# Routing batch 0 inside the last attention items, the shared expert of chunk 1 behind the routed blocks, and one closing step for the last chunk

## The reference, cut to what matters

```python
x = _layernorm(x + _L1_attn_ref(x, ...))            # heads of 16, causal softmax
# _L1_ffn_ref
scores = softmax(einsum('th,eh->te', xf, gate_w))   # 8 experts
topk_w, topk_i = top_k(scores, 2)
topk_w = topk_w / sum(topk_w)
y = sum over the 2 chosen experts of topk_w * (silu(xf @ wg[e]) * (xf @ wu[e])) @ wd[e]
shared = silu(xf @ sg) * (xf @ su) @ sd             # every token
x = _layernorm(x + y + shared)
```

## Time and profile before

| | |
|---|---|
| median of 3 runs (lowest to highest) | 717.64 us (717.23 to 723.69) |
| profiled execution | 718.89 us, of it 717.1 us span |
| PE busy in the span | 648.1 us, 90% |
| DVE busy | 412.5 us, 58% |
| ACT busy | 394.5 us, 55% |
| POOL busy | 233.0 us, 32% |
| mean granted clock of PE | 0.931 |

### The profile page before, as it was taken

The page is one execution under the profiler, slowest core; times in us unless marked ns, Lnnn a source line. Parts: engine busy times, 40 slices in busy tenths (PEclk is TensorE's granted clock), DMA queues, the critical chain, the costliest instruction groups (busy, mean ns, idle before and its releaser), DMA issues. The chain is left out here.

```text
span 717.1 us, 11088 instructions
## 1 busy us (share of the span) xinstructions
PE 648.1 (90%) x3717; PEld 301.7 (42%) x3717; DVE 412.5 (58%) x1069; ACT 394.5 (55%) x565; POOL 233.0 (32%) x255
## 2 busy tenths in 40 slices
PE   4998899999998979999969999999999889999870
PEld 1654422222431344445422222243344657877450
DVE  1478616334466696979451333245738846547697
ACT  1235679988586832545438888867775133333100
POOL 0002533335412223113341344523122705325250
PEclk9998599999998989879898999999999999999996
DMA  8500143333224422310415545433570253575331
GB/s 276 168 0 16 43 74 54 58 57 57 39 37 68 67 71 70 67 53 1 67 32 86 83 79 84 81 64 62 90 225 1 97 190 126 175 235 164 102 119 59
DMA packets 52105, 62.68 MB, mean 87 GB/s; under 512 B 10150, under 2 KB 38819, under 8 KB 51891
## 3 DMA queue, kind: packets, MB, share of 16 engines
q1 hardware_dynamic: 48971, 53.50, 33.1%
q0 software_dynamic: 3072, 8.39, 3.8%
HBM read 28.79 MB, written 18.35 MB: 66 GB/s over the span
## 5 line engine op out<-in xcount | busy, mean ns | idle before, releaser
L1411 ACT ACTIVATE probs<-ps 128x1024 f32<-128x1024 f32 (+1 forms) x320 | 276.2, 963 | 67.6 <-PE ps L1329 67.5
L1329 PE MATMUL ps<-ops_mem 99*128 99x512 bf16 (+3 forms) x768 | 165.7, 338 | 10.8 <-issue 6.8
L1346 PE MATMUL ps<-probs,vstat 128*32 128x512 f32 (+3 forms) x1536 | 169.0, 512 | 7.1 <-DVE raw L1251 6.3
L1422 POOL TENSOR_SCALAR_AFFINE_SELECT probs<-probs 128x512 f32<-128x512 f32 x128 | 84.6, 661 | 210.6 <-ACT probs L1411 210.0
L1329 PEld LDWEIGHTS ps<-ops_mem 99*128 99x128 bf16 x768 | 58.3, 99 | 159.8 <-ACT probs L1411 86.3
L1251 DVE COPY raw<-ps 128x512 f32<-128x512 f32 x32 | 22.1, 691 | 141.9 <-PE ps L1346 141.7
L1346 PEld LDWEIGHTS ps<-probs,vstat 128*32 128x32 f32 x1536 | 31.3, 109 | 70.9 <-issue 47.6
L2278 PE MATMUL ps<-parts_mem 128*128 x184 | 47.4, 381 | 0.3 <-ACT parts_mem L2159 0.3
L2122 POOL DMA_INDIRECT yT<-made,w1qkv x32 | 30.5, 954 | 47.0 <-DMA made<-parts_mem 37.8
L2113 POOL DMA_INDIRECT sent<-xres,w1qkv x32 | 30.8, 964 | 39.8 <-DVE w1qkv L615 22.2
L1720 PE MATMUL ps<-ops_mem,w1qkv 128*128 128x512 f32 x64 | 36.4, 698 | 0.1
(11 more groups left out here) (214 smaller groups left out, 937.3 us busy)
## 6 DMA issues: line engine op xcount, KB each, us to landing
ops_mem<-parts_mem SPq DMA_DIRECT2D x276, 64.0 KB
sent<-in_zero_row SPq DMA_DIRECT2D x2, 2944.0 KB, 67.9
made<-parts_mem SPq DMA_DIRECT2D x46, 128.0 KB, 1.8
probs<-sent SPq DMA_DIRECT2D x4, 896.0 KB, 8.8
ops_mem<-parts_mem SPq DMA_DIRECT2D x66, 32.0 KB
yT<-in_xT SPq DMA_DIRECT2D x4, 512.0 KB, 7.6
xres<-in_x SPq DMA_DIRECT2D x1, 2048.0 KB, 14.5
parts_mem<-in_wgu SPq DMA_DIRECT2D x2, 1024.0 KB
```

The lines of the kernel that those rows point to most:

```text
L1329: last = nc.tensor.matmul(ps[:, bank, o:o + CH - lo], kT[0:KDIM, buf, h if kh == GH else 0, kt * P:(kt + 1) * P], qT[0:KDIM, buf, h, c * C ...
L1346: last = nc.tensor.matmul(ps[32 * h:32 * h + 32, AV, lo:CH], vstat[:, i % 2, kt, h if kh == GH else 0, :], probs[:, s % PRING, h, 0:CH - l ...
L1411: nc.scalar.activation(o, banks, ACT.Exp, scale=score_scale).then_inc(s_exp, 1)
L1422: nc.gpsimd.affine_select(out=block_, in_=block_, compare_op=ALU.is_ge, fill=0.0, base=0, pattern=[[0, GH], [1, P]], channel_multiplier=-1 ...
```

## The change

It does three things.

1. **Batch 0 is routed within the attention.** The uses of bank 7 move to earlier steps: the second projection of chunk 1 from (5, 6) to (5, 4), the turns of chunk 0 from (5, 11) and (6, 2) to (5, 10) and (6, 2), its logits stay at (6, 4), the turns of chunk 1 come at (6, 6) and (6, 8) and its logits at (6, 10), in place of (6, 11), (7, 2) and (7, 4). `shift` moves behind them into item 6, ACT's `exp` from (7, 8) to (7, 1), `choose` before `take(7, 0)`, `rank` to (7, 8) in bank 7 as use 10, and `keep_rank` and `seat` before `take(7, 1)`. For this the norm of chunk 1 moves from the middle of item 6 to the end of item 5, ahead of both copies of chunk 0's turned rows. The three small tensors that `rank` and `seat` read are loaded ahead of the experts' weights, under a semaphore of their own.
2. **The shared expert of chunk 1** (`gate_up` 2 and 3, `down` 1, with their silu, product and sum) moves from before the blocks to behind them. `weigh(1)` comes into the loop at iterations 43 and 44, and chunk 0's weighing, statistics and scaling come two iterations earlier.
3. **The last chunk** ends in one sum, one norm and one store of four tiles. Weighing now comes ahead of the shared expert's sum for chunks 1 to 3, and takes the residual in with its first product.

The diff, cut to its core:

```diff
             def beside(self, pe, i, s):
-                for m, steps in enumerate((((4, 8), (4, 10)), ((5, 2), (5, 6)))):
+                for m, steps in enumerate((((4, 8), (4, 10)), ((5, 2), (5, 4)))):
                     if (i, s) in steps:
                         self.project(pe, m, steps.index((i, s)))
-                for m, steps in enumerate((((5, 11), (6, 2)), ((6, 11), (7, 2)))):
+                for m, steps in enumerate((((5, 10), (6, 2)), ((6, 6), (6, 8)))):
                     if (i, s) in steps:
                         self.turn(pe, m, steps.index((i, s)))
-                if (i, s) in ((6, 4), (7, 4)):
+                if (i, s) in ((6, 4), (6, 10)):
...
+                if (i, s) == (7, 8):
+                    pe.wait_ge(self.s_chosen, 1)
+                    pe.wait_ge(s_rank_w, 48)
+                    self.seven(pe, self.RANKS)
+                    self.rank(pe, 0, 7).then_inc(self.s_seven, 1)
             def before(self, dve, i):
                 if i == 5:
                     self.sum(dve, 1, 0)
+                    self.sum(dve, 1, 1)
                 if i == 6:
-                    self.of.k.then(self.of.statistics(0, y_sums[1]))
-                if i >= 6:
-                    self.evicted(dve, self.LOGIT[i - 6])
-                    self.keep_logits(i - 6, 7).then_inc(self.s_evicted, 1)
+                    self.keep_turned(dve, 0, 1)
+                    self.keep_seven(dve, 0)
+                if i == 7:
+                    self.choose(dve, 0)
             def between(self, dve, i):
...
                 if i == 5:
-                    self.sum(dve, 1, 1)
-                if i in (5, 6):
                     self.of.scale()
-                    self.of.apply(x_of(i - 5)).then_inc(self.s_norm, 1)
-                    self.keep_turned(dve, i - 5, 0)
+                    self.of.apply(x_of(0)).then_inc(self.s_norm, 1)
+                    self.norm(dve, 1)
+                    self.of.k.then(self.of.statistics(0, y_sums[1]))
+                if i == 6:
+                    self.keep_turned(dve, 1, 0)
+                    self.keep_turned(dve, 1, 1)
+                    self.keep_seven(dve, 1)
+                    self.shift(dve, 0)
                 if i == 7:
-                    self.shift(dve, 0)
-                    self.choose(dve, 0)
+                    self.evicted(dve, self.RANKS)
+                    self.keep_rank(7).then_inc(self.s_evicted, 1)
+                    dve.wait_ge(self.s_evicted, self.RANKS + 1)
+                    self.seat(dve, 0)
             def behind(self, dve, i):
...
                 if i == 5:
-                    self.norm(dve, 1)
-                if i in (5, 6):
-                    self.keep_turned(dve, i - 5, 1)
+                    self.of.scale()
+                    self.of.apply(x_of(1)).then_inc(self.s_norm, 1)
+                    self.keep_turned(dve, 0, 0)
...
-                        if route and (i, s) == (NI - 1, 8):
+                        if route and (i, s) == (NI - 1, 1):
                             route.exp(act, 0)
...
                 route.exp(act, 1)
-                silu(2)
-                silu(3)
...
                 bank_free(pe)
+                route.seven(pe, route.RANKS + 1)
                 project(2)
                 pe.wait_ge(s_exp_w, 16 * len(expert_weights))
-                route.rank(pe, 0)
...
                 logits(3)
-                gate_up(2)
-                gate_up(3)
-                down(1)
...
+                gate_up(2)
+                gate_up(3)
                 gate_up(4)
+                down(1)
                 gate_up(5)
...
                 route.shift(dve, 1)
-                multiplied(2)
-                multiplied(3)
                 route.choose(dve, 1)
-                accumulate(1)
                 for n in range(NB_ALL + 2):
...
-                    if n == 38:
+                    if n == 36:
                         weigh(0, (0, 1))
+                    if n == 37:
+                        weigh(0, (2, 3))
                     if n == 39:
-                        weigh(0, (2, 3))
-                    if n == 41:
                         of = normalised(0, range(CT))
                         statistics(of)
+                    if n == 41:
+                        scaled(of, 0)
                     if n == 43:
-                        scaled(of, 0)
+                        weigh(1, (0, 1))
+                    if n == 44:
+                        weigh(1, (2, 3))
+                multiplied(2)
+                multiplied(3)
                 multiplied(4)
-                weigh(1, range(CT))
+                accumulate(1)
                 multiplied(5)
...
-                for n, (lo, hi) in enumerate(LAST):
...
-                    weigh(3, range(lo, hi))
-                    of = normalised(3, range(lo, hi))
-                    statistics(of)
-                    scaled(of, 3)
+                weigh(3)
+                accumulate(3)
+                of = normalised(3, range(CT))
+                statistics(of)
+                scaled(of, 3)
```

More of the change, by code:

```diff
@@ L2367, in _, with weigh @@
                 end = Count(dve, s_dve_end)
-                def weigh(c, tiles):
+                def weigh(c, tiles=range(CT)):
                     dve.wait_ge(s_back[c], 16 * CT * TOP)
-                    if c < NC - 1:
-                        dve.wait_ge(s_dve_tail, dve_at["sum", c])
                     for k in range(TOP):
@@ L2414, in _ @@
                     if n == 3:
-                        route.keep_rank(dve, 1)
+                        dve.wait_ge(route.s_ranked, 1)
+                        route.k.then(route.keep_rank(5))
                     if n < NB_ALL:
@@ L2437, in _ @@
                 multiplied(6)
+                weigh(2)
                 accumulate(2)
-                weigh(2, range(CT))
                 multiplied(7)
```

104 lines of the change are left out of this document (48 added, 56 removed).

## The result

The changed kernel took 729.94 us (median of 20 runs, 721.83 to 734.12) against 721.43 us for the kernel before beside it: ratio 1.0131, 95% interval 1.0099 to 1.0163. On the median of 717.64 us that is 9.4 us more (7.1 to 11.7); 10.7 had been forecast. The ratio is estimated from the executions that ran at the usual clock, and is not the quotient of the two medians (1.012). On another chip, later, the same two kernels gave 1.0181 (1.0146 to 1.0215). The profiled execution has a span of 728.4 us, 11.3 more than before.

What follows compares the result with a forecast made beforehand. PE bounds layer 1's attention and the blocks, DVE the end; 8.8 + 3.7 - 12.1 + 2.7 + 1.5 + 1.7 + 4.4 = +10.7 us on 717.64 gives 728.3 us, range 721 to 734 leaving out 2 in 10.

Steps and rivals of the forecast that it cites:

- The wait at (6, 2): Attention: PE waits 6.5 us at chunk 0's second turn for a copy standing behind chunk 1's scale and apply.
- Rival B: No long wait at (6, 2), the turn needing only chunk 0's norm: 714.3 us, or down to 709.9; chance 0.06.
- Item 7: Attention: PE waits 2.3 us before the values of step 4, as `choose` stands before `take(7, 0)`.
- PE's clock: Lower clock behind the two attention waits: 2.4 us behind (6, 2), 1.3 us behind item 7, 3.7 together.
- Rival A: Waits come, but the clock does not fall and DVE catches up in the loop: +5.2, 722.8 us; chance 0.22.
- the four terms: Attention: waits of 6.5 and 2.3 us plus clock terms of 2.4 and 1.3 us.
- Ahead of the blocks: From `gate_up` 2 to the first block: chunk 1's shared expert moved away saves 12.1 us.
- The scatter: POOL's scatter of batch 0 and the first block load finish before PE reaches the blocks, hidden by 5 us.
- The first blocks: PE waits 2.7 us for ACT's copy, then DVE's `hidden`, with `choose` uncovered; 1.5 us of lower clock added.
- `weigh(1)` in the loop: Blocks near the loop's end: two halves of `weigh(1)` cost PE 1.7 us, bounds 0.6 and 3.4.
- The end: Behind the blocks: +3.1 us to DVE's last instruction and +1.3 us for the larger store, 4.4 together.
- Rival C: Lower clock lasts 3 us at each of three places, `weigh(1)` uncovered, gathered rows late: +17.2, 734.8 us; chance 0.12.

Runs made afterwards that it cites:

- experiment 1: Kernel after with both copies of chunk 0's turned rows ahead of chunk 1's scale and apply on DVE; ratio to before 0.9968.
- experiment 5: On top of experiment 1: in item 7 `choose` behind `take(7, 0)`, rank one scores step later, `seat` ahead of the last `normalise`; ratio to before 0.9970.
- experiment 10: Experiment 8 with the item 7 reordering of experiment 5 taken back, `choose` again ahead of `take(7, 0)`; ratio to before 0.9922.
- experiment 11: The repetition: kernel after once more, unchanged, on one chip with experiment 12; ratio to before 1.0181.
- experiment 12: Experiment 9's kernel once more, on one chip with the kernel after; ratio to before 1.0049.
- part 1 alone: Kernel before with only the routing of batch 0 moved into the attention; ratio to before 1.0217, +15.6 us.
- experiment 9: Kernel after with PE repeating the scores of step (6, 3) 27 times in the wait at (6, 2); ratio to before 1.0103.
- Experiment 4: Kernel after with part 1 taken back, leaving parts 2 and 3; ratio to before 0.9999.
- experiment 6: Kernel after with PE repeating the scores of step (6, 3) 17 times in the wait at (6, 2); ratio to before 1.0159.
- experiment 3: Kernel before with only part 3's single closing (sum still ahead of weighing); ratio to before 0.9971, -2.1 us.
- experiment 7: Experiment 1 with chunk 1's shared expert back ahead of the blocks, one closing kept; ratio to before 0.9947, -3.8 us.
- Experiment 8: Experiment 5 with `gate_up` 2 and 3 back ahead of the blocks, only `down` 1 behind them; ratio to before 0.9933, -4.8 us.

## Why the prediction was right

**The wait at (6, 2)**: 6.5 us forecast, 6.41 measured, on the copy and for the reason given. (The prediction's 512.15 is 512.12 by its own terms, which changes nothing.) Rival B is out: the turn did not run at once, and with the copies put first (experiment 1), which makes B's case but for item 7, the time is 717.64 - 2.3 = 715.3 us, where B gave 714.3.

**Item 7**: 2.3 us of wait forecast, 1.33 measured. Most of the difference is `choose`: DVE did it from 546.61 to 550.48 + 0.22, 4.1 us, where the step took 4.7 from the earlier trace rows. The wait made no difference that the runs can tell (experiments 5 and 10).

**PE's clock**: 2.4 and 1.3 us forecast. The first term was too small. Against the profile of before, which lost 1.6 us behind the logits itself, it measured 3.2, and 4.5 in the repetition; against work that does not fall at all, 4.8 to 6.1. Its bound of 3 us came from a low stretch of which only 6 us had been seen. The second was 0 in one execution and 1.5 in another. Rival A, no fall, is out: the fall is in the trace at (6, 2), experiments 11 and 12 show that it costs time, and A's 722.8 us, a ratio of 1.007, lies below both intervals. Together the four terms made 12.5; the stage grew by 11.7 in the profile, 0.4 of it for rank, and part 1 alone cost 15.6 by the runs.

The Trainium skill, TensorE: Matmul & The Clock Gate, section HAM oscillation, takes half the throttled time as the penalty and makes no deduction for idle time in it. In the wait itself (509.6 to 516.01) the granted clock was 0.75 on average, so part of it was low; yet the wait, which DVE ends, was as long as with PE busy at 1.00 in experiment 9 (6.41 us against 6.48). Only the work behind it grew. The measurement decides for the prediction's way of counting, though not for its size.

**Ahead of the blocks**: -12.1 forecast, -12.7 measured; the first block at 590.45, with 3.3 us of the profile's offset in it. The scatter was hidden, as forecast: the first block load was issued at 584.60, 5.9 us ahead of the first block. Experiment 4 shows that this holds only with part 1.

**The first blocks**: 2.7 us of wait and 1.5 of clock forecast, 4.2 together. Measured: a wait of 1.01 us on ACT, where before it was 0.33, and none on `hidden`. From the first block's turn to rank it took 9.5 us against 5.8, +3.7, so some 3 us of it is the lower clock. That the slow products are what let DVE catch up was not tested; in experiments 1 and 6 PE did wait for `hidden`, 0.24 and 0.40 us. The sum was right, its division was not: the two terms cover each other.

**`weigh(1)` in the loop**: 1.7 forecast; the rest of the blocks grew from 78.3 to 79.4, 1.1 us. The term stood for PE waiting for the weighing, and that is not where it went: PE's waits there went from 4.9 to 5.1 us only, and its busy time grew by 1.0 (73.3 to 74.3). A wait of 2.08 us at 671.85 is followed by products of 1.44 and 1.82 us in place of 1.03; before, a wait of 2.31 us at 669.21 was followed by one product of 2.01 us in place of 1.29.

**The end**: +4.4 forecast, +4.1 measured; DVE's last instruction 725.09 - 679.37 = 45.7 us behind the blocks, 45.9 forecast, and the store 3.3 us where 3.4 was forecast. (The prediction's 27.5 us for DVE's last stretch add up to 27.3 by its own terms.) But the heading it stood under was wrong. One closing shortens the end by 5.4 us in the profile (experiment 3); chunk 1's work, moved there, lengthens it by 49.0 - 39.5 = 9.5. So part 2 removes 12.7 us ahead of the blocks and puts 9.5 behind them and 3.7 to 4.9 into them: nothing is left, as experiments 4 and 7 say.

**Why the terms came to the right sum.** By stages, forecast and profile are +12.5 and +11.7 for the attention, -12.1 and -12.7 ahead of the blocks, +5.9 and +4.9 for the blocks, +4.4 and +4.1 for the end: 10.7 and 8.0 together. The runs gave 9.4, and 13.0 the second time, so the forecast lies between the two measurements. The big terms, the wait, the work moved and the end, were right for their reasons. Inside the stages there was luck: the clock behind (6, 2) was 1 to 2 us too small against a kernel before that loses 1.6 us there itself, and up to 4 against one that does not, while item 7 was 1 us of wait and 1.3 of clock too large, and in the blocks a wait too large by 2 stood beside a clock term too small by 1.5. The second measurement is nearer to the larger clock term. Rival C had the mechanism of the longer fall, but at all three places and with the other covers gone as well; its +17.2 us lies above both measurements.

**What beats both kernels.** Copies first, one closing, half of chunk 1 ahead of the blocks (experiment 10): ratio 0.9922 (0.9897 to 0.9947), 712.0 us on the median of before. Experiment 8 is level with it.

Two things stay open. Experiment 9 should lie above experiment 1 by about its repeats, 6.2 us of work. It lies 9.7 us above it, and its repetition, experiment 12, 5.8 (7.4 and 3.5 above the kernel before); each is known to some 3 us, and what more there is to the spread is not explained. And whether the 1 us of item 7 arrives in the runs was not found out.

## What to carry to other kernels

When an operation is moved among steps on one engine, follow the buffer that it frees: here two copies of 0.7 us, put behind 4 us of scaling, held a bank that TensorE needed, and nothing could make the time up. Count such a wait of the busiest engine at up to double its length, since the work behind it runs slower; and measure each part alone and taken back alone, because two parts may be without gain alone (part 2) or be worth only as cover for another (part 1).

## What was unexpected of the hardware

The granted clock falls in different places from one execution of the same program to the next: behind the wait of 1.3 us in item 7 it fell in two profiles (1.64 and 1.69 us for eight values) and not in five others (1.06 or 1.07). It also falls behind the narrow logits, with no long wait near. Of the ten profiles without a long wait at (6, 2), four have a fall of some 1.6 us behind the logits of chunk 0 and six have none. And `down(0)`, which follows logits of 8 columns and a wait of 1.16 us, took 3.70 us in seven of the fourteen profiled executions and 5.07 to 6.42 in the other seven; in three of these the logits themselves were already slow (2.59 to 2.76 us in place of 1.95). Whether there the narrow products or the short wait ahead of them bring it about was not tested.

Single profiles of this kernel therefore differ by some 3 us in stages that are alike, and a term of that size needs repeated runs. Over a longer stretch it is more: PE's 2588 instructions ahead of the change, which are alike in all fourteen kernels, took 479.8 to 488.4 us in the profiles.

Filling the wait of 6.4 us with useless products made the kernel faster than leaving TensorE idle in it: by 1.3% on a common chip, and by 0.3%, which is not clear of zero, in a comparison across chips. Filling it in part (3.97 us, 2.50 left) showed no gain.
